# Cross-attention and expert FFN on one core: the experts' input turned by transposing DMAs from block 2 on

## What is computed

```python
x = x + xattn(layernorm(x), ctx, ctx, Wq, bq, Wk, bk, Wv, bv)       # softmax(q k^T / sqrt(128)) v
h = layernorm(x)                                                    # the experts' input
probs = softmax(h @ router_w.T)                                     # 8 experts
a_h = gelu(h @ actor_w1.T + actor_b1)                               # 50 wide
sampled_k = argmax(clip(a_h @ actor_w2.T + actor_b2, -30, 30)) + 1  # of 6
scores = where(rank(probs) < sampled_k, probs, 0)
for e in range(8):                                                  # hidden width 336
    y = (silu(h @ gate_w[e].T) * (h @ up_w[e].T)) @ down_w[e].T
    out = out + scores[..., e:e+1] * y
x = x + out
```

## Time and profile before

| | us |
|---|---|
| median of 3 runs (lowest, highest) | 814.08 (812.65, 814.83) |
| the profiled execution: its own time | 812.56 |
| the profiled execution: span of its instructions | 810.8 |

### The profile page before, as it was taken

How to read it: one execution, slowest core, us unless ns; L and a number is a source line. 1 busy time by engine, 2 the same in 40 slices (tenths; PEclk the granted TensorE clock), 3 DMA queues, 4 the chain that set the end, 5 groups by cost and what they waited for, 6 DMA issues and landing times.

```text
span 810.8 us, 14159 instructions
## 1 busy us (share of the span) xinstructions
PE 784.4 (97%) x3923; PEld 394.7 (49%) x3923; DVE 627.4 (77%) x1351; ACT 596.3 (74%) x1047; POOL 530.0 (65%) x621
## 2 busy tenths in 40 slices
PE   7598999999999999999999999999999999999997
PEld 4344454454545545454554545455454544544443
DVE  4898778787787868778786877878688786867775
ACT  3587777877777787777777777777777778777664
POOL 2385667667576776757767575776757676676663
PEclk9689999999999999999999999999999999999999
DMA  7100001000000100000000000000000000000000
GB/s 290 39 1 13 14 6 35 1 17 23 14 27 2 38 2 13 28 13 26 0 25 15 12 26 12 26 2 25 13 12 27 1 14 1 1 14 1 13 1 27
DMA packets 20846, 17.60 MB, mean 22 GB/s; under 512 B 944, under 2 KB 19504, under 8 KB 20784
## 3 DMA queue, kind: packets, MB, share of 16 engines
q1 hardware_dynamic: 20496, 16.45, 6.4%
q10 hardware_dynamic: 288, 0.48, 0.2%
HBM read 12.73 MB, written 4.19 MB: 21 GB/s over the span
## 4 chain that ended last, share of the span: by engine, by line
PE 89%; DVE 4%; issue 3%; POOL 2%; ACT 1%; DMA 1%; DVEq 0%; POOLq 0%; ACTq 0%
PE bank L392 26%; PE bank L394 25%; PE bank L393 25%; PE bank L388 2%; PE bank L323 2%; PE bank L315 2%; PE bank L306 2%; PE bank L351 1%; POOL weighted L819 1%; PE bank L344 1%; DVE bank L1079 1%; PE bank L377 1%; DVE hid_lo L1085 1%; PE bank L294 1%; PE bank L362 1%
## 5 line engine op out<-in xcount | busy, mean ns | idle before, releaser
L819 POOL TENSOR_TENSOR weighted<-silu,score_bc 128x512 f32<-128x512 f32 x336 | 428.3, 1276 | 226.5 <-ACT silu L636 195.9
L1079 DVE SCALAR_TENSOR_TENSOR bank<-bank,h_scale,weighted 128x512 f32<-128x512 f32 x336 | 253.2, 754 | 141.0 <-PE bank L394 118.0
L630 ACT ACTIVATE hid_hi<-bank 128x512 f16<-128x512 f32 x336 | 200.4, 597 | 150.7 <-DVE bank L1079 146.0
L636 ACT ACTIVATE silu<-bank,silu_scale 128x512 f32<-128x512 f32 x336 | 230.9, 687 | 35.4 <-PE bank L394 34.2
L1085 DVE TENSOR_TENSOR hid_lo<-bank,hid_hi 128x512 f16<-128x512 f32 x336 | 228.2, 679 | 11.8 <-ACT hid_hi L630 11.7
L392 PE MATMUL bank<-xn_lo,gate_hi 128*128 128x512 f16 x336 | 128.5, 383 | 4.9 <-DVE gate_lo L909 4.9
L392 PE MATMUL bank<-xn_lo,up_hi 128*128 128x512 f16 x336 | 127.6, 380 | 0.8 <-DVE hid_lo L1085 0.7
L394 PE MATMUL bank<-xn_hi,gate_hi 128*128 128x512 f16 x336 | 128.1, 381 | 0.0
L393 PE MATMUL bank<-xn_hi,gate_lo 128*128 128x512 f16 x336 | 128.1, 381 | 0.0
L392 PE MATMUL bank<-hid_lo,down_hi 128*128 128x512 f16 x336 | 127.4, 379 | 0.6 <-DVE hid_lo L1085 0.6
L393 PE MATMUL bank<-xn_hi,up_lo 128*128 128x512 f16 x336 | 127.6, 380 | 0.0
(11 more groups left out here) (141 smaller groups left out, 839.4 us busy)
## 6 DMA issues: line engine op xcount, KB each, us to landing
x_in<-in_x SPq DMA_DIRECT2D x16, 256.0 KB, 2.6
out<-out_sb SPq DMA_DIRECT2D x16, 256.0 KB, 2.3
ctx_in<-in_ctx_t SPq DMA_DIRECT2D x16, 240.0 KB, 2.7
raw_gate<-in_gate_t SPq DMA_DIRECT2D x3, 448.0 KB, 6.4
raw_up<-in_up_t SPq DMA_DIRECT2D x3, 448.0 KB, 8.1
raw_down<-in_down_t SPq DMA_DIRECT2D x3, 448.0 KB, 9.9
consts_sb<-in_consts ACTq DMA_DIRECT2D x1, 403.0 KB, 3.7
consts_sb<-in_consts ACTq DMA_DIRECT2D x1, 64.0 KB, 4.2
```

The costliest lines, as they stand in the source:

```text
L630: af(hid_hi[j % HRING][:], up_bank[j % U_BANKS][:], ACT.Copy).then_inc(hid_hi_ready, 1)
L636: af(silu[j % RING][:], gate_bank[(par + j) % G_BANKS][:], ACT.Silu, scale=silu_scale[:])\
L819: g.tensor_tensor(weighted[j % RING][:], silu[j % RING][:], score_bc[par][:], ALU.mult)\
L1079: v.scalar_tensor_tensor(up_bank[j % U_BANKS][:], up_bank[j % U_BANKS][:], h_scale[:], weighted[j % RING][:], ALU.mult, ALU.mult).then_inc ...
```

## The change

For blocks 2 to 15 the way of the experts' input is another. ScalarE rounds the normalized `xn2_nat` to fp16 with tokens still on partitions (`token_high`, j=20 of turn n-2, behind the last `norm2`), GpSimd makes the low half (`token_low`, j=1 of turn n-1, behind `weigh` of tile 2), and the SP queue then issues two transposing DMAs, SBUF to SBUF, one for each half (128 KB each), which write `xn_hi` and `xn_lo`. `turn_x2`, `turned_x2`, `x2_high` and `x2_low` are left for blocks 0 and 1 alone. Actor and router of blocks 2 to 15 use the fp16 halves: six matmuls of 256 columns from scaled halves of `ar_t` in place of two fp32 ones. The scale is one more power of two beside those of the weights (a maximum, a few one-column operations and the two halves, made once in the setup and in turn 0), undone in the scale of ScalarE's two reads. TensorE waits for the DMAs at `actor_router_split`, now at j=4, and at `gate` of tile 0. Every later step of actor, router and scores is one j later on all engines, as are both table loads of ScalarE; `score_broadcast` and `score_spread` stay at j=19, so between `score_transposes` and `score_broadcast` there is one j where there were two. The store of a block moves from behind `out_ready` in its own turn to just ahead of the two transposing DMAs of the next turn.

```diff
             def turn(t, par):
+                if is_block(t + 1) and not by_tensor(t + 1):        # by_tensor(n): n is 0 or 1
+                    sp.wait_ge(lo_ready, t + 2)
+                    if is_block(t - 2):
+                        store(t - 2, par)
+                    turn_halves(t + 1, 1 - par)
+                elif is_block(t - 2):
+                    sp.wait_ge(out_ready, t - 1)
+                    store(t - 2, par)
                 if is_block(t + 4):
                     load_ctx(t + 4, par)
                     load_x(t + 4, par)
-                if is_block(t - 1):
-                    sp.wait_ge(out_ready, t)
-                    sp.dma_start(out_blocks[t - 1], out_sb[1 - par][:]).then_inc(stored[1 - par], 16)
...
+            def turn_halves(n, par):
+                for dst, src in ((xn_hi, xn2_hi), (xn_lo, xn2_lo)):
+                    sp.dma_start(dst[par][:].rearrange("p (b n) -> p b n", b=BB), src[:], transpose=True)\
+                        .then_inc(halves_in[par], 16)
...
+            def actor_router_split(n, par):
+                pe.wait_ge(halves_in[par], 16 * (n - par))
...
+                for w, x, first, final in ((ar_hi, xn_lo, True, False), (ar_lo, xn_hi, False, False),
+                                           (ar_hi, xn_hi, False, True)):
+                    for odd in range(2):
+                        tokens = x[par][:].rearrange("p (h s n) -> p s h n", h=2, s=2)[:, odd]
+                        last = mm(x1[odd * HALF:(odd + 1) * HALF, 0:2 * P].rearrange("p (h n) -> p h n", h=2), w[:],
+                                  tokens, start=first, stop=final)
+                last.then_inc(ah_done, 1)
...
-                    if j == 1 and is_block(t + 1):
+                    if j == 1 and by_tensor(t + 1):
                         turn_x2(t + 1)
-                    if j == 3 and is_block(t + 1):
+                    if j == 4 and by_tensor(t + 1):
                         actor_router(t + 1)
+                    elif j == 4 and is_block(t + 1):
+                        actor_router_split(t + 1, nxt)
...
-                    if j == 8 and is_block(t + 1):
+                    if j == 9 and is_block(t + 1):
                         logits(t + 1)
...
-                    if j == 17 and is_block(t + 1):
+                    if j == 18 and is_block(t + 1):
                         score_transposes(t + 1)
...
+            def token_high(n):
+                act.wait_ge(xn2_ready, n + 1)
+                af(xn2_hi[:], xn2_nat[:].rearrange("p b d -> p (b d)"), ACT.Copy).then_inc(hi_ready, 1)
...
-                    if j == 4 and is_block(t + 1):
+                    if j == 5 and is_block(t + 1):
                         actor(t + 1)
                         square(t + 1)
...
-                    if j == 9 and (is_block(t + 1) or is_block(t + 2)):
+                    if j == 10 and (is_block(t + 1) or is_block(t + 2)):
                         nc.scalar.preload_act_table(ACT.Exp)
...
-                    if j == 17 and is_block(t + 1):
+                    if j == 18 and is_block(t + 1):
                         score_copy(t + 1)
...
                     if j == 20 and is_block(t + 2):
                         norm2(t + 2, 2, BB)
+                        token_high(t + 2)
...
+            def token_low(n):
+                pool.wait_ge(hi_ready, n + 1)
+                g.tensor_tensor(xn2_lo[:], xn2_nat[:].rearrange("p b d -> p (b d)"), xn2_hi[:], ALU.subtract)\
+                    .then_inc(lo_ready, 1)
...
+                    if j == 1 and is_block(t + 1) and not by_tensor(t + 1):
+                        token_low(t + 1)
-                    if j == 3 and is_block(t + 1):
+                    if j == 3 and by_tensor(t + 1):
                         x2_low(t + 1, nxt)
-                    if j == 16 and is_block(t + 1):
+                    if j == 17 and is_block(t + 1):
                         split_scores(t + 1)
...
```

More of the change, by code:

```diff
@@ L198, in program @@
         hi_ready, lo_ready = sem("hi_ready"), sem("lo_ready")
+        ar_top_ready, ar_hi_ready, ar_ready = sem("ar_top_ready"), sem("ar_hi_ready"), sem("ar_ready")
+        halves_in = [sem(f"halves_in{k}") for k in range(2)]
         ah_done, a_ready, sq_ready, arg_ready, tanh_ready, gelu_ready, al_done, al_ready = (
@@ L229, in upto, with by_tensor @@
             return min(n + 1, BLOCKS) if isinstance(n, int) else n + 1
+        def by_tensor(n):
+            return isinstance(n, int) and n < 2
         def weight_part(n):
@@ L275, in turn @@
                     load_x(t + 4, par)
-                if is_block(t - 1):
-                    sp.wait_ge(out_ready, t)
-                    sp.dma_start(out_blocks[t - 1], out_sb[1 - par][:]).then_inc(stored[1 - par], 16)
             turns(sp, turn)
+            sp.wait_ge(out_ready, BLOCKS)
+            store(BLOCKS - 1, 1)
             for par in range(2):
@@ L353, in actor_router @@
                 last.then_inc(ah_done, 1)
+            def actor_router_split(n, par):
+                pe.wait_ge(halves_in[par], 16 * (n - par))
+                if isinstance(n, int) and n == 2:
+                    pe.wait_ge(ar_ready, 1)
+                wait(pe, kt_ready, upto(n + 1))
+                wait(pe, out_ready, n - 2)
+                for w, x, first, final in ((ar_hi, xn_lo, True, False), (ar_lo, xn_hi, False, False),
[5 more added lines that the diff above has]
+                last.then_inc(ah_done, 1)
             def probs_transposes(n, dst=x1):
@@ L412, in gate @@
                     pe.wait_ge(w_mul_ready, 1)
-                if j == 0:
+                if j == 0 and by_tensor(t):
                     pe.wait_ge(hi_ready, t + 1)
                     pe.wait_ge(lo_ready, t + 1)
+                elif j == 0:
+                    pe.wait_ge(halves_in[par], 16 * (t - par))
                 if isinstance(t, int) and t == 0 and j % PART == 0:
@@ L550, in norm2 @@
                 act.wait_ge(ln2_shift, n + 1)
-                wait(act, t2_done, n)
+                if isinstance(n, int) and n == 2:
+                    act.wait_ge(t2_done, 2)
+                else:
+                    act.wait_ge(lo_ready, n)
                 for b in range(lo, hi):
@@ L581, in actor @@
                 wait(act, gelu_ready, n)
-                af(a_sb[:], x1[:, 0:2 * P], ACT.Identity, bias=b1_col).then_inc(a_ready, 1)
+                if isinstance(n, int) and n == 2:
+                    act.wait_ge(ar_ready, 1)
+                af(a_sb[:], x1[:, 0:2 * P], ACT.Identity, bias=b1_col,
+                   scale=1.0 if by_tensor(n) else ar_scale[:]).then_inc(a_ready, 1)
             def square(n):
                 act.wait_ge(a_ready, n + 1)
-                af(x1[:, 0:2 * P], x1[:, 0:2 * P], ACT.Square, bias=b1_root[:], scale=sq_scale[:]).then_inc(sq_ready, 1)
+                af(x1[:, 0:2 * P], x1[:, 0:2 * P], ACT.Square, bias=b1_root[:],
+                   scale=sq_scale[:] if by_tensor(n) else ar_root[:]).then_inc(sq_ready, 1)
             def tanh(n):
@@ L687, in turn @@
                         norm2(t + 2, 2, BB)
+                        token_high(t + 2)
+                    if isinstance(t, int) and t == 0 and j == 5:
+                        actor_high()
                     if isinstance(t, int) and t == 0 and j == 0:
@@ L742, in _ @@
             g.memset(ones_col[:], 1.0).then_inc(setup_pool, 1)
-            for k in range(3):
+            for k in range(4):
                 g.memset(w_half[:, k:k + 1], W_TOP[k] / 2).then_inc(setup_pool, 1)
-            pool.wait_ge(setup_pool, 8)
+            pool.wait_ge(setup_pool, 9)
             pool.wait_ge(consts_in, 16)
```

77 lines of the change are left out of this document (49 added, 28 removed).

## The result

The changed kernel takes 840.18 us, the median of 4 runs (839.28 to 842.32); the kernel before, run beside it on the same chip, takes 813.37 (812.05 to 814.83). The ratio is 1.033, its 95% interval 1.030 to 1.036: 3.3% slower. The profiled execution spans 839.1 us, 28.3 more than that of before.

A forecast was written before the change was run, and what follows sets the result against it. TensorE's dense stream was taken to bound the kernel. -7.6 + 0.6 + 33.3 = +26.3 us on the profiled 812.56 gives 838.9; the runs' median stands 1.5 higher, so 840.4 us, range 808 to 880.

The forecast's parts named there:

- TensorE's work: TensorE's stream, blocks 2 to 15: 1.11 us leaves, 0.57 comes, 0.54 saved per block; -7.6 us (-2.9 at the other end).
- the wait for the DMAs: TensorE at j=4: 11 turns stall by 5.1 - 2.97, three seam turns by 5.1 - 1.8; +33.3 us.
- the later steps one j on: Steps after j=4 move together and keep their distances, with two exceptions; price 0, at worst 0.3 per turn, 4 us.
- setup and turn 0: About eight small operations join VectorE and ScalarE, where TensorE waits for VectorE; +0.6 us, from nothing to 1.5.
- When TensorE comes: TensorE reaches the new wait at j=4 5.91 us after j=1, in turn 7 at 392.14.
- when the low half is ready: GpSimd's `token_low`, behind `weigh` of tile 2, is done at 389.17 in turn 7; slack 2.97 us.
- At the loop's seam: Turns 6, 8 and 10: ScalarE stands 1.35 us, `weigh` of tile 2 starts late; slack 2.05 or 1.50, taken as 1.8.
- What the DMAs need: SP queue, low half to landing: wake 0.2, store 0.8, two halves 2.6 in 256-byte rows, fixed 1.5; 5.1 us.
- Plain transfers: Rival at the j=4 wait: transposing DMAs cost what others do, 3.3 us; sum +1.1, 815.2 us; chance 0.14.
- Faster: Rival at the j=4 wait: low half lands within 2.5 us, only seam turns stall; sum -4.9, 809.2 us; chance 0.13.
- Slow, or the clock: Rival: DMAs need 7.7 us, stall 69.7, 877 us; or shorter stalls lower TensorE's granted clock; chance 0.13.
- the prediction's signs: TensorE idle before the first actor matmul, 2 us and more at turns 6, 8, 10; turn 49.5 us; clock 1.00.

The follow-up runs named there:

- run 5: Changed kernel with the high half's transposing DMA issued early and the later actor, router and score steps back at their old j: 809.67 us, ratio 0.995.
- run 1: Kernel before, old turning and no transposing DMA, with the later actor, router and score steps and table loads one j later: 823.77 us, ratio 1.012.
- run 3: Changed kernel with the high half's transposing DMA issued when that half is ready, ahead of the store and the low half's: 817.45 us, ratio 1.005.
- Run 8: run 1's kernel with GpSimd's `route_probs` and `count_less` back at j=11, ahead of the `weigh` that the table loads delay: 814.47 us, ratio 1.000.
- runs 9 and 10: First: run 3's kernel with Run 8's edit, 807.79 us. Second: run 5's kernel with the halves of `ar_t` made at the end of turn 0, 806.63 us.

## Why the prediction was right, and where two errors cancelled

The time was right, 840.4 against 840.18, and so was the main mechanism, TensorE waiting at j=4 for the DMAs. The sum was not: a stall too large by 11 us and a squeeze of the later steps too small by 11. That the total came out within 0.3 us is luck.

| term | predicted | measured |
|---|---|---|
| TensorE's work | -7.6 | -7.4 |
| the wait for the DMAs | +33.3 | +22.6 |
| the later steps one j on | 0 (at worst 4) | about +11 |
| setup and turn 0 | +0.6 | +1 to 2.8 |

The measured terms add up to 27.2 to 29.0; the profiled spans differ by 28.3, the medians by 26.8.

**TensorE, right.** 1.12 leaves per block, and the six half-width passes cost 0.57: they cost 0.54 alone, and 0.59 with `turn_x` behind them (1.03 - 0.44). They do run side by side: at 0.11 from one pair to the next, two of 256 columns take the time of one.

**When TensorE comes and when the low half is ready, right** within 0.1: a slack of 2.88 against 2.97. **At the loop's seam, wrong.** There should have been 1.8 in turns 6, 8 and 10. Turn 8 is such a turn, and there `weigh` of tile 2 starts 0.66 behind TensorE's j=1 (450.66 - 450.00), where it was 1.47 before. ScalarE's idle time ahead of `high` of tile 20 at the seam is gone, and not because TensorE became the later one: in run 5, where TensorE has no stall, it is gone too, and in run 1, which keeps ScalarE's old steps at that place, it is still there, at the start of turn 8:

```profile
440.22 0.60 ACT L630 ACTIVATE hid_hi<-bank 128x512 f16<-128x512 f32 x1 [1.41 <-PE bank L394]
```

It went with ScalarE's new list, which has `token_high` just there; why is open. What sets the loop's turns apart after the change is something else, and all of them alike: from the low half to the matmul 4.62 to 4.67 us in turns 4 to 11, 4.25 to 4.28 in turns 2, 3, 12 and 14. Of the difference 0.15 lies between the low half and the store's issue and 0.2 between the last issue and the matmul; in both places the loop's waits go by a register's value. That this is the cause was not tried. (Turns 1 and 13 have 4.5, with a longer way from the last issue to the matmul.)

**What the DMAs need, wrong in its terms.** I had 0.2 + 0.8 + 2.6 + 1.5 = 5.1, transfers one after the other. It was issues one after the other: 0.18 until the store, 0.46, 1.26, then 2.5 to the landing and 0.2 to the matmul, 4.6. The pieces are of 256 bytes, as supposed: 35,728 - 20,496 = 15,232 packets more, 544 for each of the 28 DMAs; in the trace 512 of them have 256 bytes and 32 have 4. But one costs less than the queue's mean packet: 0.085 x 16 x 839.1 less 830 engine-us is 311, by 28 and 16 engines 0.69 us per DMA, not 1.3. That is the step which failed: I took a packet's cost from larger ones, added the transfers of the store and the high half, which are over when the low half's begins, and took the issue of a DMA as 0.4 us whatever its kind. With 14 turns, 4.6 or 4.3 for 5.1, and no seam, the stall comes to about 22.6, which is the sum of the step's cost over all turns less its cost without a stall (1.03, run 3).

**The steps after j=4, wrong,** and the second step which failed: a term put at nothing that measured 11 us. "Which leaves their distances": it leaves those among the steps that move, not those to the steps of other blocks that stay, and to these belong `attend`'s sums (L1077), the statistics (L1016) and `result` (L1154) on VectorE. I followed ScalarE's table loads to TensorE's `gate` 15, which does hold, and not into the other two engines. The timeline of VectorE after the change, turn 7, shows where they went:

```profile
426.86 0.68 DVE L1069 TENSOR_TENSOR v_sb<-bank,consts_sb 120x512 f32<-120x512 f32 x1
...
430.98 1.23 DVE L1136 TENSOR_SCALAR al_far<-al_less 128x24 f32<-128x24 f32 x1 [0.94 <-POOL al_less L858]
...
437.68 0.86 DVE L1016 BATCH_NORM_STATS2 stats<-x_all 128x6 f32 x4
438.46 0.17 DVE L1147 SCALAR_TENSOR_TENSOR score<-rank_less,prob 128x32 f32<-128x32 f32 x1
...
440.09 0.65 DVE L1154 TENSOR_TENSOR out_sb<-bank,x_all 128x512 f32<-128x512 f32 x1
```

In the kernel before the loads end at 409.74 and `keys` starts at 425.13, 15.4 us later; VectorE needs 15.0 of them to catch up as far as `result`, which `keys` waits for (424.69). After the change the loads end at 427.35 (ScalarE's timeline, the instruction behind the second)

```profile
427.35 0.60 ACT L691 ACTIVATE hid_hi<-bank 128x512 f16<-128x512 f32 x1
```

and TensorE would be ready for the scores at 439.56 + 0.216 + 0.09 = 439.87 and for `keys` 0.41 later, at 440.28: 12.9 us, over a tile less. `result` ends at 440.74. VectorE also stands still for 0.94 of that time, waiting for `al_less`, since a step of the other kind left the stretch: the copy of `values`, which stays at its place, lay behind the loads before (411.75, the row of VectorE's timeline of the kernel before below) and lies ahead of their end now (426.86, above).

```profile
411.75 0.68 DVE L987 TENSOR_TENSOR v_sb<-bank,consts_sb 120x512 f32<-120x512 f32 x1
```

And `score` comes behind the statistics, which it preceded before. Run 8 took the 0.94 away, by having GpSimd make `al_less` ahead of the `weigh` that the loads delay by 3.25, and got 0.69 of the 0.79 back. Of `score_broadcast` I was right: 0.43 for 0.41.

**Setup, too low.** From the start to the end of turn 0 the changed kernel needs 2.8 us more; as the kernels of runs 1 and 8, with the same setup, differ by 1.2 at their first `score_broadcast` (40.57 and 41.73), I can't say more than 1 to 2.8.

**The rivals.** *Plain transfers* came nearer to the transfer (0.4 us there, 1.3 in the forecast, 0.69 measured) and was wrong about the queue, like the forecast. The Trainium skill (Advanced Engine Details and Errata, X-Bar Transpose (TRN2)) has transposing DMAs as fast as regular ones; the trace agrees nearly as to landing (2.6 against 2.2 us), and not as to the issue (1.2 against 0.5 to 0.6) or the transfer itself (205 to 212 GB/s against 277 to 328). *Faster* would have needed 3.05 us or less; even plain copies took 2.88 + 0.64 = 3.5 in the loop from the low half to the matmul, near the 3.3 of the rival of that name. *Slow, or the clock*: the granted clock was 1.00 in the turn read above, through a stall of 1.75 us. Of the prediction's signs, the turn of 49.5 us came as 49.9 in the loop, and the longer stalls at turns 6, 8 and 10 did not come.

Not tried: the edit of run 8 on the changed kernel with its stall, and both of runs 9 and 10 together.

## What to carry to other kernels

A DMA's price on a waiting path is its landing plus every issue that stands between the data's readiness and its own: issue each as soon as its own operand is there, and keep stores and independent halves out from between. When a chain of steps is moved as a whole, check its distances to the steps that stay, on each engine, above all behind a long stall such as a table load. And a total that comes out right proves no term of it; here two terms were wrong by 11 us each, and only runs with one part of the change each showed it.

## What the runs showed of the hardware

- A transposing DMA of 128x512 fp16 from SBUF to SBUF occupies the SP queue for about 1.2 to 1.3 us; a plain copy of the same size 0.51 to 0.60, a plain store of 256 KB to HBM 0.40. It landed 2.5 to 3.6 us after its issue (median 2.6; in run 3 2.4), a plain copy 2.0 to 3.1 (median 2.2).
- It moves in 512 packets of 256 bytes and 32 of 4, and takes each of the 16 DMA engines for about 0.69 us: 0.020 us per packet, half of the queue's mean before. While it moves, the core's rate is 205 to 212 GB/s; with the plain copies it is 277 to 328.
- Six matmuls of 256 columns, three each into output partitions 0 to 63 and 64 to 127, take 0.54 us of TensorE's stream with their edges.
- The same wait for the same transfers cost TensorE about 0.4 us more in the loop's turns 5 to 11 (2.78 to 2.84) than in the written-out turns 2, 3 and 12 (2.35 to 2.42); in turns 1, 4 and 13 it was 2.60 to 2.70.
